# Experts: down products in float32r passes, one accumulator, three sets of gate and up banks

## What is computed

```python
scores = sigmoid(x @ gate_w.T);  choice = scores + gate_bias
# two of four groups of experts by the sum of their best two; of these the best eight
w = take(scores, topk_idx);  w = 2.5 * w / (w.sum() + 1e-20)
g, u = x @ expert_gate, x @ expert_up            # for every expert, 64 inner columns each
outs = (silu(g) * u) @ expert_down
final = sum over the eight chosen of outs * w
shared = (silu(x @ shared_gate) * (x @ shared_up)) @ shared_down
return final + shared
```

## Time and profile before

| | us |
|---|---|
| median of 3 runs | 3079.76 (3079.65 to 3083.96) |
| span of the profiled execution | 3079.5 |
| PE busy | 2914.8 (95%) |
| PEld, loading weights | 2276.4 (74%) |
| DVE busy | 2223.1 (72%) |
| ACT busy | 1577.7 (51%) |
| POOL busy | 1182.6 (38%) |
| experts | about 1643 to 2323 |

### The profile page before, as it was taken

One profiled execution on the slowest core, in us unless ns is written; L12 is line 12 of the kernel. 1 busy time (PEld: TensorE's weight loads), 2 busy tenths in 40 slices (PEclk: granted clock), 3 DMA queues, 4 the chain that ended last, 5 costly groups with the idle time before them and its releaser, 6 DMA issues. The chain is left out here.

```text
span 3079.5 us, 89598 instructions
## 1 busy us (share of the span) xinstructions
PE 2914.8 (95%) x34642; PEld 2276.4 (74%) x34642; DVE 2223.1 (72%) x5778; ACT 1577.7 (51%) x2906; POOL 1182.6 (38%) x1274
## 2 busy tenths in 40 slices
PE   7999799999998999869997999999998999999978
PEld 6888545555556888747776888888886888888864
DVE  7777666666654666668887777788776788878766
ACT  6777321112114777537774333333335777777756
POOL 6777200000004777554540000000004677777753
PEclk9999899999998999979998999999998999999989
DMA  5000266666551000011111333332330000000001
GB/s 159 19 10 8 70 194 185 180 181 178 168 169 35 12 10 10 2 53 26 26 25 57 112 104 104 104 98 97 104 112 16 12 10 10 8 10 10 10 1 55
DMA packets 110871, 212.03 MB, mean 69 GB/s; under 512 B 18737, under 2 KB 30449, under 8 KB 110194
## 3 DMA queue, kind: packets, MB, share of 16 engines
q1 hardware_dynamic: 110194, 209.03, 23.0%
q10 hardware_dynamic: 512, 0.92, 0.1%
HBM read 198.34 MB, written 5.77 MB: 66 GB/s over the span
## 5 line engine op out<-in xcount | busy, mean ns | idle before, releaser
L384 PE MATMUL ps<-parts 128*128 128x512 f32 (+3 forms) x1568 | 624.2, 398 | 33.0 <-DVE parts L1002 18.6
L385 PE MATMUL ps<-parts 128*128 128x512 f32 (+3 forms) x1568 | 565.6, 361 | 0.0
L386 PE MATMUL ps<-parts 128*128 128x512 f32 (+3 forms) x1568 | 563.8, 360 | 0.0
L318 POOL TENSOR_TENSOR rstd<-mv,eps 128x4 f32<-128x4 f32 x106 | 21.2, 200 | 999.1 <-DVE mv L301 999.1
L1945 ACT ACTIVATE work<-ps 128x512 f32<-128x512 f32 x272 | 162.4, 597 | 443.2 <-PE ps L386 442.9
L384 PEld LDWEIGHTS ps<-parts 128*128 128x128 f32 (+2 forms) x1568 | 299.4, 191 | 105.3 <-ACT work L837 26.3
L582 POOL TENSOR_TENSOR work<-work 128x512 f32<-128x512 f32 x256 | 266.9, 1043 | 275.0 <-DVE work L972 275.0
L386 PEld LDWEIGHTS ps<-parts 128*128 128x128 f32 (+2 forms) x1568 | 299.2, 191 | 46.4
L385 PEld LDWEIGHTS ps<-parts 128*128 128x128 f32 (+2 forms) x1568 | 301.4, 192 | 20.7
L1910 PEld LDWEIGHTS ps<-early,work 128*128 128x128 f32 x2176 | 281.8, 192 | 18.9 <-DVE pause L1999 0.3
L1910 PE MATMUL ps<-early,work 128*128 128x128 f32 x2176 | 288.4, 276 | 0.1
(11 more groups left out here) (296 smaller groups left out, 6074.7 us busy)
## 6 DMA issues: line engine op xcount, KB each, us to landing
work<-gate_rows SPq DMA_DIRECT2D x128, 512.0 KB, 5.6
work<-expert_rows SPq DMA_DIRECT2D x512, 128.0 KB, 3.0
work<-gate_rows SPq DMA_DIRECT2D x128, 256.0 KB, 7.0
work<-in_ctxT SPq DMA_DIRECT2D x72, 192.0 KB, 2.4
out<-x SPq DMA_DIRECT2D x16, 256.0 KB, 2.3
work<-work SPq DMA_DIRECT2D x224, 16.0 KB
work<-work SPq DMA_DIRECT2D x16, 128.0 KB, 2.3
early<-in_l0f_w SPq DMA_DIRECT2D x1, 1536.0 KB
```

Of the source, the lines that this page charges most:

```text
L384: T.matmul(out, lh, rh, start=True, stop=False)
L385: T.matmul(out, lh, rl, start=False, stop=False)
L386: return T.matmul(out, ll, rh, start=False, stop=True)
```

## The change

The down products become float32r passes like the others: stationary are the high and low parts of the down weights (`wdh`, `wdl`), moving are the high and low parts of the activations (`ah`, `al`), 512 columns each, three passes per block, into one accumulator `acc` that holds the transposed result. High parts are made by ACT (`take_high`), low parts by POOL (`take_low`), for each block. After block 16 ACT copies the accumulator to `yT` (`take_sum`, step 0 of the next group), PE turns it back with four transposes into `ps_x` (`turn_back`, step 4), and DVE adds it to x (`add`, step 5). There are three banks for gate and three for up, so PE runs `gate_up` of block j+3 in step j; `down` is done for block j-1. ACT's `silu` and DVE's blocks move to j+3 as well, `take_high` and `take_low` treat block j+2.

The split of hT moves from DVE to ACT (high) and POOL (low). The scaling of `hn` moves from DVE to two POOL instructions in step 13, its moments to step 12. The routing's parts are spread over steps 2 to 10 (`PARTS`); `turn_weights` stays in step 11. At the head the low parts of the second piece of the gate and up weights and of the whole down weights are made by POOL, and PE's main loop waits for all three. `wb` and `hT`, `yT` lie in the region of the original weights. The first two groups are written out ahead of the loop.

```diff
+def by_pairs_and_first(eng, n, body):
+
+    body(0, 0, False)
+    body(1, 1, False)
+    if n > 4:
+        with eng.Fori(1, n // 2 - 1) as it:
+            body(it * 2, 0, False)
+            body(it * 2 + 1, 1, False)
+    body(n - 2, 0, True)
+    body(n - 1, 1, True)
...
-    WR = 8
-    w = c.carve()
+    WR, NS, NA = 8, 3, 5
+    w, e = c.carve(), c.carve(c.early[:, 3 * W2N:])
+    spent = c.carve(c.early[:, 0:2 * W2N])
     hn = c.hn
-    hT = [w([GT]), w([GT])]
+    hT, yT = [e([GT]), e([GT])], e([GT])
     r = c.carve(c.parts)
     hTh, hTl = [r([GT]), r([GT])], [r([GT]), r([GT])]
-    wgh, wgl, wuh, wul = (r([W2N]) for _ in range(4))
-    sg, aT = [w([GT]), w([GT])], [w([GT]), w([GT])]
-    wT, wb = [w([GT]), w([GT])], [w([GT]) for _ in range(WR)]
+    wgh, wgl, wuh, wul, wdh, wdl = (r([W2N]) for _ in range(6))
+    ah, al = [r([GT]) for _ in range(NA)], [r([GT]) for _ in range(NA)]
...
+    sg, aT = [w([GT]) for _ in range(NS)], [w([GT]) for _ in range(NS)]
+    wT, wb = [w([GT]), w([GT])], [spent([GT]) for _ in range(WR)]
...
-    ps_g, ps_u = (tuple(c.ps[:, i + j, :] for j in range(2)) for i in (0, 2))
-    acc, ps_x = (c.ps[:, 6, :], c.ps[:, 4, :]), c.ps[:, 7, :]
+    ps_g, ps_u = ([c.ps[:, i + j, :] for j in range(NS)] for i in (0, NS))
+    acc, ps_x = c.ps[:, 6, :], c.ps[:, 7, :]
...
+    PARTS = ((0,), (1,), (2,), (3,), (4, 5), (6,), (7,), (8, 9), (10, 11, 12))
+
+    def ahead(g, u, j, k):
 
         return (g, u, j + k) if j + k < NB else (g + 1, 1 - u, j + k - NB)
 
-    def at(g, u, j):
-
-        return g * NB + j, (u + j) % 2
+    def number(g, j):
+        return g * NB + j
+
+    def bank(j):
+
+        return j % NS
+
+    def before_bank(g, j):
+
+        m = number(g, j)
+        return m - 3 if j >= NS else (m - 2 if j < 2 else m - 5)
...
+            def weights_low(low, src, high, ready):
+                pool.wait_ge(w_high, ready)
+                G.tensor_tensor(low, src, high.bitcast(FP), ALU.subtract).then_inc(rest_low, 1)
+
+            def split_low(g, u):
+
+                pool.wait_ge(high_ready, g + 1)
+                G.tensor_tensor(hTl[u], hT[u], hTh[u].bitcast(FP), ALU.subtract).then_inc(low_ready, 1)
+
+            def scale_rows(g):
+
+                pool.wait_ge(norm.rstd_ready, g + 1)
+                pool.wait_ge(x_ready, g * 3 - 2)
+                G.tensor_tensor(hn, norm.xg(g), bc(c.mv[:, :, 0], 2, D), ALU.subtract).then_inc(centred, 1)
+                pool.wait_ge(centred, g)
+                G.tensor_tensor(hn, hn, bc(c.rstd[:, 0:TG], 2, D), ALU.mult).then_inc(norm.ready, 1)
+
+            def take_low(g, u, j):
+
+                pool.wait_ge(a_high, number(g, j) + 1)
+                G.tensor_tensor(al[part(j)], aT[bank(j)], ah[part(j)].bitcast(FP), ALU.subtract).then_inc(a_low, 1)
+
+            split_low(0, 0)
+            for ready, low, high, name in ((3, wgl, wgh, "l2f_g"), (4, wul, wuh, "l2f_u")):
+                weights_low(low[:, pieces[1]], c.w[name][:, pieces[1]], high[:, pieces[1]], ready)
+            norm.rstd(pool, 1)
+            weights_low(wdl, c.w["l2f_d"].rearrange("p j c -> p (j c)"), wdh, 5)
+            scale_rows(1)
+            for j in range(2):
+                take_low(0, 0, j)
+
+            def body(g, u, last_pair):
+                end = last_pair and u == 1
+                for j in range(NB):
+                    if not (end and j + 2 >= NB):
+                        take_low(*ahead(g, u, j, 2))
+                    if j == 1 and not end:
+                        split_low(g + 1, 1 - u)
+                    if j == 12 and not last_pair:
+                        norm.rstd(pool, g + 2)
+                    if j == 13 and not last_pair:
+                        scale_rows(g + 2)
+                    if end and j in (9, 10):
+                        nxt.rstd(pool, j - 9)
+
+            by_pairs(pool, n, body)
...
-            def down(g, u, j):
-                m, b = at(g, u, j)
-                te.wait_ge(a_ready, m + 1)
+            def down(g, j):
+                k, cols = part(j), slice(j * P, (j + 1) * P)
+                te.wait_ge(a_low, number(g, j) + 1)
                 if j == 0:
-                    need(te, added, g)
+                    need(te, y_out, g)
+                T.matmul(acc, wdh[:, cols], ah[k], start=(j == 0), stop=False)
+                T.matmul(acc, wdl[:, cols], ah[k], start=False, stop=False)
+                T.matmul(acc, wdh[:, cols], al[k], start=False, stop=(j == NB - 1)).then_inc(down_done, 1)
+
+            def turn_back(g):
+
+                te.wait_ge(y_out, g + 1)
                 for t in range(TG):
-                    last = T.matmul(acc[u][:, t * D:(t + 1) * D], aT[b][:, t * P:(t + 1) * P], c.w["l2f_d"][:, j, :],
-                                    start=(j == 0 and t == 0), stop=(j == NB - 1), skip_group_check=True)
-                last.then_inc(y_ready if j == NB - 1 else down_done, 1)
+                    last = T.transpose(ps_x[:, t * D:(t + 1) * D], yT[:, t * P:(t + 1) * P], c.w["ident"][:, :])
+                last.then_inc(yt_ready, 1)
...
+            te.wait_ge(rest_low, 3)
 
             def body(g, u, last_pair):
                 end = last_pair and u == 1
+                head = isinstance(g, int) and g == 0
                 for j in range(NB):
-                    if not (end and j + 2 >= NB):
-                        gate_up(*ahead(g, u, j))
+                    if not (end and j + NS >= NB):
+                        gate_up(*ahead(g, u, j, NS))
                     if j == 0 and not end:
                         transposes(g + 1)
                     if j == 1 and not end:
                         router(g + 1, 1 - u)
+                    if j == 4 and not head:
+                        if end:
+                            te.wait_ge(x_out, n * 3)
+                        else:
+                            te.wait_ge(x_out, g * 3 + 5)
+                        turn_back(g - 1)
                     if j == 11 and not end:
                         turn_weights(g + 1, 1 - u)
-                    down(g, u, j)
-
-            by_pairs(te, n, body)
+                    if j:
+                        down(g, j - 1)
+                    elif not head:
+                        down(g - 1, NB - 1)
+
+            by_pairs_and_first(te, n, body)
+            down(n - 1, NB - 1), turn_back(n - 1)
...
+            def take_high(g, u, j):
+
+                act.wait_ge(a_ready, number(g, j) + 1)
+                if known(g, j, before_part):
+                    act.wait_ge(down_done, before_part(g, j) + 1)
+                A.activation(ah[part(j)], aT[bank(j)], ACT.Copy).then_inc(a_high, 1)
...
+            def take_sum(g):
+
+                act.wait_ge(down_done, g * NB + NB)
+                need(act, yt_ready, g)
+                A.activation(yT, acc, ACT.Copy).then_inc(y_out, 1)
...
+                    if not (end and j + NS >= NB):
+                        silu(*ahead(g, u, j, NS))
                     if not (end and j + 2 >= NB):
-                        silu(*ahead(g, u, j))
+                        take_high(*ahead(g, u, j, 2))
                     if j == 0 and not end:
                         take_hT(g + 1, 1 - u)
+                    if j == 0 and not head:
+                        take_sum(g - 1)
                     if j == 1 and not end:
-                        sigmoid_exp(g + 1)
+                        sigmoid_exp(g + 1), split_high(g + 1, 1 - u)
                     if j == 11 and not end:
                         take_weights(g + 1, 1 - u)
 
-            by_pairs(act, n, body)
+            by_pairs_and_first(act, n, body)
...
-                out.then_inc(u_read, 1)
+                b = bank(j)
+                ve.wait_ge(silu_ready, number(g, j) + 1)
+                if known(g, j, before_bank):
+                    ve.wait_ge(a_low, before_bank(g, j) + 1)
...
-            def split(g, u):
-
-                ve.wait_ge(x_out, g * 3 + 1)
-                split_high(c, hTh[u], hT[u]).then_inc(high_ready, 1)
-                ve.wait_ge(high_ready, g + 1)
...
+                    if not (end and j + NS >= NB):
+                        block_of(*ahead(g, u, j, NS))
+                    if j == 5 and not head:
+                        add(g - 1)
+                    if 2 <= j < 11 and not end:
+                        for part_ in PARTS[j - 2]:
+                            routing(g + 1, 1 - u, part_)
+                    if j == 12 and not last_pair:
                         norm.take_moments(ve, g + 2)
-                    if j == 11 and not last_pair:
-                        norm.scale(ve, g + 2)
                     if end and j == 9:
-                        ve.wait_ge(x_ready, n)
+                        ve.wait_ge(x_ready, n * 3 - 2)
                         nxt.take_moments(ve)
                     if end and j == 10:
```

(42 more changed lines are left out.)

76 lines of the change are left out of this document (38 added, 38 removed).

## The result

The changed kernel takes 3229.3 us (median of 4 runs, 3228.8 to 3229.9) against 3079.7 for the kernel before on the same chip: ratio 1.048, 95% interval 1.0467 to 1.0493. It is slower, by 150 us; 3199 was predicted, with a range of 3067 to 3255.

A forecast was written before the change was run, and what follows sets the result against it. PE was taken to bound the kernel before, at 41.2 us a group. On 3079.5, 15 groups at +5.8 (87), last group, head and tail (4) and clock (29) gave +120: 3199 us, range 3067 to 3255.

The forecast's parts named there:

- rival 1: Experts' groups: DVE and POOL take turns reading SBUF; 3199 us, between 3128 and 3255; chance 0.71.
- the named signs: PE waiting 4 to 6 us at weights' transposes, passes 0.45 apart behind, wb product 0.69 to 1.9, groups 47 to 50.
- router to turn, no collision: PE's router to the turning of the weights: chain through ACT, DVE blocks and routing, weights ready at 25.4 us.
- collisions on that stretch: DVE's blocks and routing between router and turn wait for POOL's SBUF reads: 24.3 against 20.0, +4.3 us a group.
- turn to router, no collision: PE's own work from turning the weights to the next router: 15.2 us a group.
- clock, late POOL, semaphores: Per group: clock loss, 1.5 us for POOL late to the next group's first blocks, rounding up to 47.0 for semaphores.
- The clock: PE at half speed some 5.9 us after the turn's stall, losing 2.9, in two groups of three: 29 us.
- the risk of the three banks: ACT's new waits: silu of block m+2 queues behind take_high of block m, which waits for DVE's product with wb.
- Head and tail: Low parts moved to POOL delay the head by 6 us (-1 to +9); tail +2.7; last group without routing -5.
- The turn stall alone: No collisions in the groups, or POOL takes all waits; 3074 us, 3067 to 3082; chance 0.15.
- PE as the bound: Routing reaches the turning of the weights in time, 4.2 us less a group; 3020 us; chance 0.10.
- The clock staying low: PE's clock doesn't recover between several waits a group, a step takes 4.1 us; 3500 us; chance 0.04.

The follow-up runs named there:

- the first experiment: Changed kernel with DVE's first product written back to up's PSUM bank, where the product with wb reads it; 3136.2 us, ratio 1.0173.
- the kernel with the turn in step 12: Changed kernel with the product with wb reading its operand from PSUM, plus turning and copying of the weights in step 12 instead of 11; 3089.0 us, ratio 1.0036.
- the best: Changed kernel with wb product reading from PSUM, weights turned in step 12, and all 16 groups written out without a loop; 3070.4 us, ratio 0.9969.
- the kernel with the filled turn: Changed kernel with PE turning the unit matrix 32 times before its wait for the routing's result; 3202.0 us.

## Why the prediction was right, and by how much it was off

The direction, the mechanism (rival 1) and the size held; 28 us of 148 were missing. Of the named signs only the length of a group misses, 50.9 where 47 to 50 was said. By where the time lies: from the end of the head's stall to the last update of x it is 801.4 us after (1670.4 to 2471.8) and 658.3 before (1663.7 to 2322.0), +143.1; the head itself +6.8, and what comes behind -2.3. The forecast had 87 + 29 - 5 + 2.7 = +113.7 for the first and +6 for the second. So the 28 are in the groups, about 2.0 each.

| step, us a group | forecast | measured |
|---|---|---|
| router to turn, no collision | 25.4 | 25.2: 26.36 with the operand in PSUM, less 1.12 that is still collision |
| of it PE's wait | 3.6 | 3.28 |
| collisions on that stretch | +4.3 | 30.33 - 25.24 = +5.1 |
| turn to router, no collision | 15.2 | 15.2: 17.42 with the operand in PSUM, less half clock 1.8 and a wait for hT 0.4 |
| clock, late POOL, semaphores | 1.9 + 1.5 + 0.6 = 4.0 | 19.88 - 15.2 = 4.7 |
| the loop's turn | 0 | 2.3 in every second group, 1.15 |
| sum | 48.9 | 51.3 in the two groups from 1875.6 to 1978.1 (the column, without the wait, adds up to 51.4); 50.9 in the mean of 13 |

**Down products.** A step of nine passes is 2.05 apart where PE isn't stopped (an L384 at 1981.91, the same of the next step at 1983.95), as forecast, and nothing of it shows in the time: the loop of router, routing and turn sets the group. That was the heart of the forecast, and the wait of 5.4 at L1974 (4 to 6 forecast), which two different edits take down to 0.3 and 0 with 62 and 65 us, shows it.

**The collision** was read off two stretched instructions of another layer. Its price, 4.3 + 1.5 a group, stands against 6.1 between the changed kernel and the first experiment's; the interval of a block was to be 2.61, and `take_low` starts 2.55 to 2.58 apart. The waits fall on DVE for the most part, as taken: L2129 gains 0.42 in the mean, `take_low` 0.06. The parts of the routing collide as well, and go on doing so with the operand in PSUM. From the kernel with all groups written out, DVE and POOL:

```profile
1767.34 0.93 DVE L2159 TENSOR_TENSOR work<-work 128x16 f32<-128x16 f32 x1
...
1766.94 1.29 POOL L1932 TENSOR_TENSOR parts<-work,parts 128x512 fp32r<-128x512 f32 x1 [0.23 <-ACT parts L2063]
```

The addition of 128x16 ends 0.04 behind POOL's instruction; the same addition takes 186 to 192 ns in the kernel before. It comes once a group, and so does the tensor_scalar L2140, 0.60 where it takes 0.22 in the kernel before: 0.74 and 0.38 are the 1.12 of the table.

**The clock.** Passes were at half speed behind all 15 turns that have groups before them, until 2.5 to 5.5 us after PE resumed, 4.2 in the mean, where two groups in three were assumed. At the forecast's 2.9 each that would have been 44; at half of 4.2 it is 32, and filling the wait gave back 27. The forecast's 29 came out by luck: the frequency was too low and the price of one too high.

**What was missing.** First the loop's turn, a term that the forecast had at nothing: 16 us of the 28, by writing the groups out. The rows that I read before held it (9.0 us "issue" at L1995), but in a kernel with 9 us of slack a group on DVE it cost little, 6 us in all, and I passed over it as idle time of an engine that isn't the bound. The change put DVE's chain on the path, though DVE is busy only 365 of 500 us there, and the gap went with it. Second, the collisions, 0.8 above the forecast on the stretch from router to turn; the rest of that stretch is as forecast (25.2 against 25.4; first silu behind the table loads ends 5.5 after the router, forecast 5.4; from there DVE needs 24.8 to the last part of the routing, collisions included, forecast 24.3). Third, PE waits 1.7 us for hT before the router. ACT's `take_hT` stands in its queue behind `take_high`, and that behind DVE's product: the queueing that I had named as the risk of the three banks, but priced only for the first blocks.

**Head and tail.** PE resumed at 1670.42, forecast 1671; POOL's 7.46 for two pieces of 1664 and 4.76 for the 2176 columns compare with 8.0 and 5.3 taken. The way there is the one forecast, routing and POOL taking turns: two small instructions of the routing, 0.19 and 0.22 in the kernel before, wait out POOL's two subtractions, and POOL then waits for the moments that come behind the routing:

```profile
1652.08 2.61 DVE L2153 TENSOR_TENSOR work<-work 128x16 f32<-128x16 f32 x1
1654.72 3.70 DVE L2158 TENSOR_TENSOR work<-work 128x64 f32<-128x64 f32 x1
...
1664.35 0.20 POOL L318 TENSOR_TENSOR rstd<-mv,eps 128x4 f32<-128x4 f32 x1 [6.01 <-DVE mv L301]
```

At the tail PE waits 2.0 and 2.9 us for `take_low`, in its last steps, behind the next layer's scaling of `hn` on DVE, of which four instructions take 2.08 and 3.03: they are tensor_scalars with one operand from SBUF (L359), 0.33 alone and 1.28 to 1.32 where `take_low` runs. Even so the ends come out as forecast: 143.1 less 15 groups of 9.7 is -2.4, and -5 + 2.7 = -2.3 was taken.

**The rivals.** The turn stall alone (3074) falls with L2129's spread, but its number is what the kernel with the turn in step 12 comes near, 3089, by another way. PE as the bound (3020) is reached by no variant: the best has groups of 40.05, 3.0 above PE's own 37.0, and its turn still waits 1.2 us for the routing. The clock staying low (3500) falls with 1.00 over 1965 to 1970.

## What to carry to other kernels

Before giving an idle GpSimd work that reads SBUF, look for VectorE instructions with two SBUF operands in the same loop, and for a chain that starts the one at the end of the other; if one operand can be left in PSUM, that product's collision is gone. Look at the tensor_scalars too: here those with a single operand from SBUF were stretched to three times their length. When an engine comes from slack onto the path, everything in its queue that cost nothing comes due, the gap at the turn of a loop included: add its idle time that is put down to nothing to the sum. A late result is worth one later step for its consumer (47 us here), but spreading the work that makes it stays better than bunching it once the lateness is gone.

## What the runs showed of the hardware

- VectorE stops at the turn of a repeated body of two groups: 3.27 us of idle time put down to nothing in the kernel with the turn in step 12, 2.4 us on the length of such a group (43.1 against 40.6), 9.0 us over four turns in the kernel before. Written out, all 16 groups and all five engines, it is gone, with 6, 16 and 19 us gained. The Trainium skill (Advanced Engine Details and Errata, Control Flow Timing) gives some 108 ns for a compare-and-branch; the measured gap is some twenty times that, so it isn't the branch alone. What it is made of wasn't tried.
- A VectorE product of two SBUF operands waits up to 1758 - 691 = 1067 ns for a running GpSimd instruction, and GpSimd up to 1818 - 1261 = 557 ns for it; small operands don't escape (128x16: 0.19 us alone, 0.90 at the least in the loop; 128x64: 0.22 alone, 3.70 beside a subtraction of 1664 columns). With one operand in PSUM all 256 stay within 691 to 694 ns.
- A single operand from SBUF isn't enough to be safe: VectorE's tensor_scalar of 128x128 takes 342 ns alone and 1054 to 1197 in all 60 instances beside additions of GpSimd (L310), 0.33 and 1.28 to 1.32 at the changed kernel's tail (L359), 0.22 and 0.60 in its routing with the operand in PSUM (L2140).
- Behind a wait of PE of 3.28 us the granted clock fell to half in 12 of 15 groups, in the one shown about 1 us after PE resumed and until about 4.4 us after. It fell also behind waits of at most 1.9 us before the router, in 12 of 15 groups of the kernel with the filled turn; with the turn in step 12, where no wait of PE is longer than 1.5 us, it stayed at 1.00.
